# Turning the low-rank projection round in layers 1 and 3 of a four-layer StyleGAN/LoRA stack: split weights stationary, y's two parts moving

## The reference

```python
# layer 0: 8 routed adapters of rank 16 (softmax of 8 logits)
# layer 1: y @ kernel + bias + the sample's adapter + a shared adapter, each of rank 32
z = y @ A.T            # (rows, 32 + 32): own adapter (mixed by the gate), shared adapter
out = y @ W + bias + z @ B.T
# layer 2: y @ W.T + top 2 of 28 adapters of rank 8
# layer 3: H = y @ W.T + b; z = y @ A (rank 32); a mix of 8 experts weighs z at the end
delta = ((z * p_mix) @ Bmat) * scaling    # p_mix needs maxima over all rows
```

## Time and profile before

| what | value |
|---|---|
| median of 3 runs | 1902.27 us (1899.55 to 1908.01) |
| profiled execution, its own time | 1907.9 us |
| its span, first to last instruction | 1906.1 us |
| PE busy | 1778.4 us, 93% |
| PE weight loads busy | 1476.4 us, 77% |
| DVE busy | 839.0 us, 44% |
| ACT busy | 665.4 us, 35% |
| DMA queue q1 | 35.8% of 16 engines |
| mean granted TensorE clock | 0.956 |

### The profile page before, as it was taken

One profiled execution on the slowest core, in us unless ns is written; L12 is line 12 of the kernel. 1 busy time (PEld: TensorE's weight loads), 2 busy tenths in 40 slices (PEclk: granted clock), 3 DMA queues, 4 the chain that ended last, 5 costly groups with the idle time before them and its releaser, 6 DMA issues.

```text
span 1906.1 us, 25849 instructions
## 1 busy us (share of the span) xinstructions
PE 1778.4 (93%) x9128; PEld 1476.4 (77%) x9128; DVE 839.0 (44%) x2329; ACT 665.4 (35%) x1237; POOL 58.1 (3%) x99
## 2 busy tenths in 40 slices
PE   5888998978999999999899999999989999999995
PEld 4777777767888888887688888888777888888873
DVE  5154555554333334355543444434564333333327
ACT  2355555433333333334432323323253333332310
POOL 2000000010000000001000000000102000000000
PEclk9799999968999999999999999999998999999996
DMA  6657667438333233314322222222241223222218
GB/s 123 129 127 166 141 151 156 116 86 105 83 80 91 55 91 80 86 46 134 110 76 65 66 75 59 78 64 56 69 117 45 64 77 84 75 80 70 65 43 331
DMA packets 227625, 181.76 MB, mean 95 GB/s; under 512 B 176184, under 2 KB 187672, under 8 KB 227294
## 3 DMA queue, kind: packets, MB, share of 16 engines
q1 hardware_dynamic: 222142, 173.35, 35.8%
q10 hardware_dynamic: 2640, 5.26, 0.9%
q0 software_dynamic: 2768, 2.13, 0.8%
HBM read 108.34 MB, written 42.99 MB: 79 GB/s over the span
## 4 chain that ended last, share of the span: by engine, by line
PE 63%; issue 23%; DVE 5%; SPq 3%; DMA 3%; ACT 2%; POOL 1%; POOLq 0%; DVEq 0%; ACTq 0%
PE ps L1000 54%; PE ps L1815 3%; SPq L1352 3%; DMA filt<-filt 2%; PE ps L1134 2%; PE ps L1086 1%; DVE w_lo L1483 1%; DMA raw<-in_L_ffn_W 1%; DVE x_last L1970 1%; DVE filt L775 0%; POOL limes_rep L1895 0%; PE ps L2027 0%; ACT w_hi L1479 0%; ACT filt L441 0%; PE ps L1835 0%
## 5 line engine op out<-in xcount | busy, mean ns | idle before, releaser
L1000 PE MATMUL ps<-xp_hi,filt 128*128 128x512 f32 x1024 | 336.2, 410 | 18.0 <-DMA filt<-filt 15.8
L1000 PE MATMUL ps<-w_hi,y_hi 128*128 128x512 f32 x768 | 312.5, 407 | 0.0
L1000 PE MATMUL ps<-w_hi,y_lo 128*128 128x512 f32 x768 | 305.4, 398 | 0.0
L1000 PE MATMUL ps<-w_lo,y_hi 128*128 128x512 f32 x768 | 304.7, 397 | 0.0
L1000 PEld LDWEIGHTS ps<-xp_hi,filt 128*128 128x128 f32 x1024 | 192.5, 194 | 62.7 <-DMA filt<-filt 15.2
L764 DVE SCALAR_TENSOR_TENSOR xp_lo<-ps,mods_pair,xp_hi 128x512 fp32r<-128x512 f32 x128 | 96.3, 752 | 276.6 <-ACT xp_hi L431 272.6
L431 ACT ACTIVATE xp_hi<-ps,mods_pair 128x512 fp32r<-128x512 f32 x128 | 88.1, 689 | 360.0 <-PE ps L1000 360.0
L1000 PE MATMUL ps<-xp_lo,filt 128*128 128x512 f32 x512 | 206.3, 403 | 0.0
L447 ACT ACTIVATE y_nat<-ps,mods_pair 128x512 f32<-128x512 f32 x128 | 99.6, 778 | 213.3 <-PE ps L1000 213.2
L1000 PEld LDWEIGHTS ps<-w_lo,y_hi 128*128 128x128 f32 x768 | 145.4, 189 | 35.3
L1000 PEld LDWEIGHTS ps<-w_hi,y_hi 128*128 128x128 f32 x768 | 146.0, 190 | 31.2
(11 more groups left out here) (317 smaller groups left out, 2879.1 us busy)
## 6 DMA issues: line engine op xcount, KB each, us to landing
x_in<-x_state SPq DMA_DIRECT2D x96, 256.0 KB, 3.9
x_res<-x_state SPq DMA_DIRECT2D x48, 512.0 KB, 3.9
x_state<-x_res SPq DMA_DIRECT2D x46, 512.0 KB, 2.9
filt<-filt SPq DMA_DIRECT2D x128, 128.0 KB, 2.7
filt<-filt SPq DMA_DIRECT2D x128, 96.0 KB, 2.5
raw<-in_x SPq DMA_DIRECT2D x16, 512.0 KB, 5.3
x_res<-in_x SPq DMA_DIRECT2D x16, 512.0 KB, 4.3
x_state<-raw SPq DMA_DIRECT2D x16, 512.0 KB, 3.8
```

The lines of the kernel that those rows point to most:

```text
L1000: ins = nc.tensor.matmul(out, st[x0], mv[x1], start=first and t == 0, stop=last and t == 2, **kw)
```

## The change

In layers 1 and 3 the sides of the projection are exchanged: the weights (64 columns in layer 1; in layer 3 hi and lo stand beside each other as 2 x 32 columns) are stationary and y_hi and y_lo (128 columns) move. The result is z.T at once, on partitions 0 to 63. The copy to z_sb and the transpose go. In layer 1 a block takes 3 products, 24 for a pair; in layer 3 it takes 2, 16 for a pair. The weights are split by ACT and DVE: all of them in the fills of layers 1 and 3, the group's own adapter once for each further group at the end of a step with j = 1 (`split_adapter_act`, `split_adapter_dve`). SP loads the adapter's first half one step earlier than before (`load_mixed_a`, at j = 0, ahead of the shift of the filters), the second half (`load_mixed_b`) where it was. y_f is written in layer 0 alone, and y_lo always comes from PSUM.

```diff
-Z_OPS = (5, 1, 16, 1)
+Z_OPS = (5, 0, 16, 0)
 # sp_step
+            if l == 1 and j == 0 and more:
+                load_mixed_a(sp, i + 1)
             if more:
                 sp_shift_filter(sp, l, n + 2)
             if l == 1 and j == 1 and more:
-                load_mixed(sp, i + 1)
+                load_mixed_b(sp, i + 1)
 # act_split_y
-                if l != 2:
+                if l == 0:
                     nc.scalar.activation(y_f[:, :, C * q:C * q + C], src, ACT.Copy).then_inc(s["act_f"], 1)
 # act_step, dve_step (behind act_tail_in, dve_tail_in)
+            if l == 1 and j == 1:
+                split_adapter_act(act, i + 1)
+            if l == 1 and j == 1:
+                split_adapter_dve(dve, i + 1)
 # dve_y_lower
-                if l == 2:
-                    src = ps[:, 3 + 2 * q, :].rearrange("p (b c) -> p b c", c=C)
-                else:
-                    dve.wait_ge(s["act_f"], whole_y(l, n, q))
-                    src = y_f[:, :, c]
+                src = ps[:, 3 + 2 * q, :].rearrange("p (b c) -> p b c", c=C)
 # pe_step, pe_drain: ahead of pe_project
             pe.wait_ge(s["dve_t"], smp(l - 1, n, 1))
-            if l in (1, 3):
-                pe.wait_ge(s["act_f"], whole_y(l, n, 1))
 # act_narrow, dve_narrow (fill of layer 3)
+                nc.scalar.activation(proj_hi[:, :, 0:32], proj_raw[:, :, 0:32], ACT.Copy).then_inc(s["adapt_act"], 1)
+                dve.wait_ge(s["adapt_act"], GROUPS + 1)
+                nc.vector.tensor_tensor(proj_hi[:, :, 32:C], proj_raw[:, :, 0:32], f(proj_hi[:, :, 0:32]),
+                                        ALU.subtract).then_inc(s["adapt_dve"], 1)
 # dve_shared, act_shared (fill of layer 1)
+            dve.wait_ge(s["adapt_act"], 1)
+            v.tensor_tensor(proj_hi[:, :, C:2 * C], proj_raw[:], f(proj_hi[:, :, 0:C]), ALU.subtract).then_inc(s["adapt_dve"], 1)
+            act.wait_ge(s["adapt_loaded"], 16)
+            nc.scalar.activation(proj_hi[:, :, 0:C], proj_raw[:], ACT.Copy).then_inc(s["adapt_act"], 1)
+        def split_adapter_act(act, g):
+            act.wait_ge(s["adapt_loaded"], 16 * g + 16)
+            act.wait_ge(s["pe_zt"], pid(1, 2 * g))
+            nc.scalar.activation(proj_hi[:, :, 0:32], proj_raw[:, :, 0:32], ACT.Copy).then_inc(s["adapt_act"], 1)
+        def split_adapter_dve(dve, g):
+            dve.wait_ge(s["adapt_act"], g + 1)
+            nc.vector.tensor_tensor(proj_hi[:, :, C:C + 32], proj_raw[:, :, 0:32], f(proj_hi[:, :, 0:32]),
+                                    ALU.subtract).then_inc(s["adapt_dve"], 1)
 # act_tail_in
+            if l == 3:
+                act.wait_ge(s["dve_zt"], pid(l, n))
+                nc.scalar.activation(z_sb[0:32, 0:P], ps[32:C, 6, 0:P], ACT.Copy).then_inc(s["act_zt"], 1)
+                return
 # dve_route
-            if l == 1:
-                done(v.tensor_copy(z_sb[:, 0:PROJ_W[l]], ps[:, 6, 0:PROJ_W[l]]), 1)
-            if l == 3:
-                done(v.tensor_copy(z_sb[:, 0:96].rearrange("p (c r) -> p c r", c=3),
-                                   ps[:, 6, 0:32].unsqueeze(1).to_broadcast([P, 3, 32])), 1)
 # dve_tail_in, l == 3
-                v.tensor_copy(zt_nat[:, ds(P * n, P)], ps[0:96, 6, 0:P]).then_inc(s["dve_zt"], 1)
+                for c in range(3):
+                    last = v.tensor_tensor(zt_nat[32 * c:32 * c + 32, ds(P * n, P)], ps[0:32, 6, 0:P], z_sb[0:32, 0:P], ALU.add)
+                last.then_inc(s["dve_zt"], 1)
 # pe_project
-            if l != 2:
-                proj = proj_0 if l == 0 else proj_raw
-                for kb in range(KB):
-                    last = nc.tensor.matmul(ps[:, 0 if l == 0 else 6, 0:PROJ_W[l]], y_f[:, kb], proj[:, kb, 0:PROJ_W[l]], ...)
+            if l == 1:
+                if j == 0:
+                    pe.wait_ge(s["adapt_dve"], i + 1)
+                for kb in range(KB):
+                    last = mm3(ps[0:C, 6, 0:P], [proj_hi[:, kb, 0:C], proj_hi[:, kb, C:2 * C]],
+                               [t[:, kb] for t in (y_hi, y_lo)], kb == 0, kb == KB - 1)
+                last.then_inc(s["pe_zt"], 1)
+            if l == 3:
+                for kb in range(KB):
+                    for r, t in enumerate((y_hi, y_lo)):
+                        last = mm(ps[0:C, 6, 0:P], proj_hi[:, kb, 0:C], t[:, kb], start=kb == 0 and r == 0, stop=kb == KB - 1 and r == 1)
+                last.then_inc(s["pe_zt"], 1)
 # pe_project_T
+            if l in (1, 3):
+                return
```

More of the change, by code:

```diff
@@ L235, in build @@
             dve_mp dve_g dve_t dve_y dve_x dve_b dve_l dve_p dve_end dve_k dve_z dve_zt dve_o dve_e
-            x_loaded e_loaded chain""".split()
+            x_loaded e_loaded chain adapt_loaded adapt_act adapt_dve""".split()
         s = {n: sem(n) for n in names}
@@ L456, in act_split_y, with whole_y @@
                     nc.scalar.activation(y_hi[:, :, C * q:C * q + C], src, ACT.Copy).then_inc(s["act_t"], 1)
-                if l != 2:
+                if l == 0:
                     nc.scalar.activation(y_f[:, :, C * q:C * q + C], src, ACT.Copy).then_inc(s["act_f"], 1)
-        def whole_y(l, n, q):
-            return smp(l if l < 2 else 2, n, q)
+        def whole_y(n, q):
+            return smp(0, n, q)
         def act_step(act, l, i, j, more, one_more):
@@ L496, in act_step @@
                     act_filter(act, l, n + 2, j)
-            if l in (1, 2):
+            if l > 0:
                 act_tail_in(act, l, n)
+            if l == 1 and j == 1:
+                split_adapter_act(act, i + 1)
             if not more and j == 0 and l + 1 == LAYERS:
@@ L1144, in pe_step_0 @@
                 pe_edge(pe, l, g_next, 1)
-            pe.wait_ge(s["act_f"], whole_y(l, n, 1))
+            pe.wait_ge(s["act_f"], whole_y(n, 1))
             pe.wait_ge(s["dve_o"], pid(l, n) + 1)
@@ L1265, in pe_drain_0 @@
             pe_transpose_y(pe, l, n + 1, False)
-            pe.wait_ge(s["act_f"], whole_y(l, n + 1, 1))
+            pe.wait_ge(s["act_f"], whole_y(n + 1, 1))
             pe.wait_ge(s["dve_o"], pid(l, n + 1) + 1)
@@ L1581, in pe_wide @@
                 pe.wait_ge(s["raw_dve"], part_count(l, NARROW_PARTS[l] + 15))
+            if l == 3:
+                pe.wait_ge(s["adapt_dve"], GROUPS + 1)
         def act_wide(act, l):
@@ L1684, in mix_store, with load_mixed_a, load_mixed_b @@
                     .then_inc(s["mix_stored"], 16)
-        def load_mixed(sp, g):
+        def load_mixed_a(sp, g):
             if is_zero(g):
                 sp.wait_ge(s["mix_stored"], 5 * 16)
+            else:
+                sp.wait_ge(s["adapt_dve"], g)
+            sp.dma_start(proj_raw[:, :, 0:32], mixed_a_dram[g].rearrange("p (k r) -> p k r", r=32)).then_inc(s["adapt_loaded"], 16)
+        def load_mixed_b(sp, g):
+            if is_zero(g):
                 sp.wait_ge(s["narrow_pe"], 1)
@@ L1704, in split_mixed_act @@
         def split_mixed_act(act, g):
-            act.wait_ge(s["mixed_loaded"], 32 * g + 32)
+            act.wait_ge(s["mixed_loaded"], 16 * g + 16)
             act.wait_ge(s["pe_o"], pid(1, 2 * g))
@@ L1745, in done @@
                 dve.wait_ge(s["dve_z"], zc(l, n, step))
-            dve.wait_ge(s["pe_z"], pid(l, n) + 1)
+            if l in (1, 3):
+                return
+            dve.wait_ge(s["pe_z"], pid(l // 2, n) + 1)
             if l == 0:
@@ L1807, in pe_project @@
         def pe_project(pe, l, i, j):
-            n = 2 * i + j
-            if l == 1 and j == 0:
-                pe.wait_ge(s["mixed_loaded"], 32 * i + 32)
-            if l != 2:
-                proj = proj_0 if l == 0 else proj_raw
+            mm = nc.tensor.matmul
+            if l == 0:
                 for kb in range(KB):
-                    last = nc.tensor.matmul(ps[:, 0 if l == 0 else 6, 0:PROJ_W[l]], y_f[:, kb], proj[:, kb, 0:PROJ_W[l]],
-                                            start=kb == 0, stop=kb == KB - 1)
+                    last = mm(ps[:, 0, 0:PROJ_W[l]], y_f[:, kb], proj_0[:, kb], start=kb == 0, stop=kb == KB - 1)
                 last.then_inc(s["pe_z"], 1)
-                return
-            for kb in range(KB):
-                last = mm3(ps[:, 6, 0:PROJ_W[l]], [t[:, kb] for t in (y_hi, y_lo)],
-                           [t[:, kb, 0:PROJ_W[l]] for t in (proj_hi, proj_lo)], kb == 0, kb == KB - 1)
-            last.then_inc(s["pe_z"], 1)
+            if l == 1:
[5 more added lines that the diff above has]
+                last.then_inc(s["pe_zt"], 1)
+            if l == 2:
+                for kb in range(KB):
+                    last = mm3(ps[:, 6, 0:PROJ_W[l]], [t[:, kb] for t in (y_hi, y_lo)],
+                               [t[:, kb, 0:PROJ_W[l]] for t in (proj_hi, proj_lo)], kb == 0, kb == KB - 1)
+                last.then_inc(s["pe_z"], 1)
+            if l == 3:
+                for kb in range(KB):
+                    for r, t in enumerate((y_hi, y_lo)):
```

(5 more changed lines are left out.)

9 lines of the change are left out of this document (1 added, 8 removed).

## The result

| | before | after |
|---|---|---|
| median of the same comparison | 1901.21 us (4 runs) | 1875.55 us (4 runs, 1872.20 to 1876.48) |
| ratio | | 0.9838 [0.9812, 0.9864] |
| span of the profiled execution | 1906.1 us | 1874.6 us |
| PE busy | 1778.4 us | 1747.2 us |
| ACT busy | 665.4 us | 643.5 us |

Forecast were 20.7 us and a time of 1882, range 1874 to 1892: the sign came true and so did the price of the pairs, the size was too small, and by the ratio the time lies just under the low end of the range.

A forecast was written before the change was run, and what follows sets the result against it. PE was taken to bound layers 1 and 3. Steady steps -20.1 us, layer 1's fill +0.7 and layer 3's last step -1.3 summed to -20.7, from 1902.3 to 1881.6, predicted as 1882 us; range 1874 to 1892.

The forecast's parts named there:

- The pair's price: New projection in layers 1 and 3: pairs of a 64-column load and 128-column fp32r stream start 0.061 us apart.
- The upper bound of 0.110: Upper end for the new pair's distance in us, from transposes with 128 columns loaded and 128 streamed.
- The lower one, 0.049: Lower end for the new pair's distance in us, from the rows' end products with 48 columns.
- rival A: New projection pairs: loads don't hide behind short streams, each pair costs both, 0.116 us; total 1914 us; chance 0.07.
- B: New projection pairs: fp32r streams 128 columns in four passes, 0.235 us; +81 us, total 1983; chance 0.04.
- C: New projection pairs: load and stream hide each other only in part, distance about 0.080 us; total 1892; chance 0.13.
- D: Whole kernel: a wait takes the gain back, PE meeting the same DMA or ACT work later; 1900 us; chance 0.03.
- What stays hidden: ACT and DVE copies, sums, adapter split and load_mixed_a in the steady steps: covered by slack, costed at nothing.
- The fill of layer 1: Start of layer 1: the new ACT copy of 512 columns stands ahead of PE's awaited chain, +0.7 us.
- Ends: Fills and last step: layer 1's fill +0.7 us, layer 3's 0 up to 0.4, layer 3's last step -1.3.
- handover: Steady steps of layers 1 and 3: from last projection pair to first w_hi product, 0.11 us kept as before.
- Waits: Steady steps: 0.2 us pause ahead of the projection, waiting for next pair's y_nat, stays; other slacks cover, no cost.

The follow-up runs named there:

- load128_l3: Changed kernel, each pair of layer 3's projection loading 128 stationary columns, 64 of them unused: 1885.1 us, one run.
- act_copies: Changed kernel with an unread ACT copy of 512 columns put back behind each y_hi half in layers 1 and 3: 1873.5 us, one run.
- late_split: bank6_wait with the split of the adapter's weights in layer 1's fill moved behind tail_hi on ACT and the first pair's xp_lo on DVE: 1868.65 us, ratio 0.9789.
- before_again: Kernel before, unedited, run and profiled a second time against itself: ratio 1.0008.
- only_l1: Kernel before with the change made in layer 1 alone: 1892.39 us, ratio 0.9951.
- moving64_l3: Kernel before with layer 3's projection moving 64 columns instead of 32, the extra results unread: 1903.94 us, ratio 0.9989.
- bank6_before: Kernel before with PE's wait for y_nat ahead of the projection split by banks, sample 1 awaited later: 1898.25 us, ratio 0.9943.
- keep_turn_l3: Changed kernel with one unread 128x128 transpose of the identity put where layer 3's transpose of z stood: 1881.3 us, one run.
- bank6_wait: Changed kernel with PE's wait for y_nat ahead of the projection split by banks, sample 1 awaited later: 1866.74 us, ratio 0.9797.
- only_l3: Kernel before with the change made in layer 3 alone: 1881.75 us, ratio 0.9894.

## Why the prediction came out right in kind and short in size

**The pair's price: right.** Forecast 0.061 us from the pairs of 64 and 64 columns, measured 0.060 in two ways, the timeline and the doubled loop. The upper bound of 0.110 was the price of a load of 128 columns, as load128_l3 shows with 0.111. The lower one, 0.049, belongs to a pair with the same load of 64 columns, and so contradicts the 0.057 that the prediction gave that load; with 16 moving columns it is 0.042. The forecast came right because its row had nearly the new pair's stream, and the stream sets the distance. By the Trainium skill, "TensorE: Matmul & The Clock Gate", section "Back-to-back issue gap", a matmul of 128 columns would have taken about 81 ns; here it takes 60 with 64 columns to load and 111 with 128. The rule of the Trainium skill, same page, Part 3, "The mechanism", that a load overlaps matmuls only where the row groups differ, would have made rival A happen; the runs disagree with it for these pairs on 128 partitions (0.060 us). The same section of the Trainium skill also lets a load go ahead where it targets a background weight buffer, which the prediction didn't weigh. B is out as well: fp32r keeps its pace at 128 columns. C and D didn't come: the distance is 0.060 and not 0.080, and no gain of the steady steps was lost to a wait.

**What stays hidden: right.** ACT's copies, the three sums, the group's split and `load_mixed_a` cost nothing in the steady steps (act_copies, and PE busy throughout; the group's split and `load_mixed_a` have no run of their own). The fill of layer 1 came at +0.64 for +0.7, and late_split confirms its cause. The fill of layer 3, forecast at 0, shows no cost (-0.16 with the drain ahead of it).

**The step that failed is "Ends", with the handover in the steady steps beside it.** "Ends" gave the last step -1.3 us beyond a steady one and the first steps nothing, and priced the clock in no place but the 16 pairs of the last step. By the table the first and last steps gave some 4.2 us more than that. In all the table has 6.8 us more than the sum of 20.7:

- *Handover, 1.9 us.* I kept 0.11 from the last pair to w_hi as "the load of 128 columns before it". Measured is 0.06: that load lies behind the streams of the last pairs. The product that follows w_hi also comes a little sooner (0.29 for 0.32 us). A step gains 0.475 and 0.944 for 0.41 and 0.87, over 28 steps.
- *First steps, 0.7 and 1.55 us.* I read "Waits" and "Ends" for waits and copies alone and took the clock of the stretch, 1.00 in the earlier trace rows, for that of each of its steps. In step 0 of layer 1 the low clock of the fill reaches into the step: over its first 6 us it is 0.54 and 0.58 in the two profiles of before, 0.75 and 0.64 after, and that makes the 0.7. As the two profiles after differ by 0.5 us here (31.57 and 32.10), how much of it is the change's isn't shown. In step 0 of layer 3 eight products behind the projection run at 1.2 GHz before, and none after. That fall is absent in all nine profiles with layer 3 turned round and present in three of the five with its plain form (before, before_again, only_l1). Yet the narrow pairs alone don't make it: moving64_l3 and bank6_before don't have it. These two are also the plain ones in which layer 1 had its falls, so where falls stand may be a matter of the single execution as much as of the edit. What triggers them stays open.
- *The last step, 2.0 us.* PE there, against the earlier trace rows:

```profile
1809.68 1.09 PE L1135 MATMUL ps<-ident,y_nat 128*128 128x128 f32 x8
1812.44 0.37 PE L1854 MATMUL ps<-y_hi,proj_hi 128*64 128x128 f32 x1 [1.67 <-DVE y_lo L849]
...
1814.10 0.31 PE L1854 MATMUL ps<-y_lo,proj_hi 128*64 128x128 f32 x1
1814.21 0.73 PE L1001 MATMUL ps<-w_hi,y_hi 128*128 128x512 f32 x1
1814.74 0.63 PE L1001 MATMUL ps<-w_hi,y_lo 128*128 128x512 f32 x1
1815.17 0.55 PE L1001 MATMUL ps<-w_lo,y_hi 128*128 128x512 f32 x1
1815.56 0.39 PE L1001 MATMUL ps<-w_hi,y_hi 128*128 128x512 f32 x1
```

The start (2.76 for 3.61 us behind the first transpose, so -0.85 for -0.6) and the pairs at half pace (1.77 for 3.29, as forecast; 2.94 in the second profile of before) are two terms. The third I hadn't priced: the clock comes back after three products of 512 columns, where before it took eight, in the second profile ten. The timeline of the kernel before, behind its first w_hi product of the earlier trace rows:

```profile
1844.46 0.63 PE L1000 MATMUL ps<-w_hi,y_lo 128*128 128x512 f32 x1
...
1847.45 0.48 PE L1000 MATMUL ps<-w_lo,y_hi 128*128 128x512 f32 x1
1847.76 0.39 PE L1000 MATMUL ps<-w_hi,y_hi 128*128 128x512 f32 x1
```

The 24 products take 6.24 (and 6.37 in the second profile) for 7.37 us (7.70). The transpose adds 0.12, as forecast, and some 0.6 lies in the end of the program, which the change doesn't touch.

It is tempting to say that the shorter pause brings the clock back sooner, but the other profiles don't bear it out. In load128_l3 the pause is 2.76 us as after, and twelve of the products run at half pace; a window of its last step:

```profile
1820.50:1826.50 6.00, 6.00 (x19) 4.94 (x19) 0.84 (x3) 0.27 (x1) 0.00 (x0) 0.50 0.00 0
```

In bank6_before it is 3.60 us as before, and the pairs took 1.81, full pace. In act_copies the pause is 3.22 us, and pairs (1.02 us) and products (5.65) all ran at full pace; so they did in keep_turn_l3, bank6_wait and late_split with the pause of 2.76. Pairs and products together take 8.0 us in the kernel after and 6.7 in these four: the clock moves this term by 1.4 us from one profile to the next, for a cause that stays open.

The other 0.7 us of the 6.8 lie in the drains and fills of the layers 1 to 3, where I had put 0 and clock steps of that size come and go.

## What to carry to other kernels

Price a short product by its distance in a stream, and look for a row with the same load and the same stream: the larger of the two sets it. Here a load of 128 columns cost 0.111 us and a load of 64 at most 0.042, below the 0.060 of a stream of 128 fp32r columns, so the narrow side belonged on the stationary side. After the steady steps have been priced, walk through the first and the last step of each layer by their own rows: there the clock's steps weighed as much as the work. And ask of a pause that a change leaves alone what its wait is for: one wait split in two gave about 5 us more here by steps 1 to 14, without the clock's part.

## What the runs showed of the hardware

- A load of 64 columns and a stream of 128 fp32r columns go on at 0.060 us a pair, over 24 pairs without a break; with 128 columns loaded, 0.111 (load128_l3). With 64 loaded and 16 plain columns moved the distance is 0.042. Plain float32 pairs with 128 columns loaded and 32 or 64 moved cost the same step, 26.11 us.
- The granted clock fell with PE 100% busy (4.00 of 4.00 us, 0.58 in that window) in step 0 of layer 3. Such falls stood in other places in other profiles, in code that hadn't been edited too (step 14 of layer 1 in moving64_l3 and only_l3). A kernel whose PE is always busy isn't free of them.
- Two executions of the same kernel differed by 7.5 us in layer 0 and by less than 0.3 us in steps 1 to 14 of each later layer; a clock fall, where one comes, adds 1.5 us (380.9 for 379.31 in layer 1). For a change of some 10 us the cut by stretch says more than one span does.
